# One product for the last FFN chunk's 64 gate rows and 64 up rows, with ScalarE moving the up rows to the gate rows' partitions

## The reference, cut to what matters

```python
g = jnp.einsum('td,edf->tef', x, wg)          # 32 experts, 96 hidden each
u = jnp.einsum('td,edf->tef', x, wu)
act = jax.nn.silu(g) * u
routed = jnp.einsum('tef,efd,te->td', act, wd, combine)
shared = jax.nn.silu(hidden_states @ sg) * (hidden_states @ su) @ sd   # 192 hidden
return routed + shared
```

## Time and the profile before

| | |
|---|---|
| median of 3 runs | 1710.79 us (1708.7 to 1717.45) |
| the profiled execution | 1712.23 us, of which its span is 1710.4 us |
| mean granted TensorE clock in it | 0.955 |
| PE busy | 1536.3 us |
| DVE busy | 1258.4 us |
| POOL busy | 982.6 us |
| ACT busy | 844.5 us |

### The profile page before, as it was taken

One profiled execution on the slowest core, in us unless ns is written; L12 is line 12 of the kernel. 1 busy time (PEld: TensorE's weight loads), 2 busy tenths in 40 slices (PEclk: granted clock), 3 DMA queues, 4 the chain that ended last, 5 costly groups with the idle time before them and its releaser, 6 DMA issues. The chain is left out here.

```text
span 1710.4 us, 22495 instructions
## 1 busy us (share of the span) xinstructions
PE 1536.3 (90%) x7088; PEld 1165.2 (68%) x7088; DVE 1258.4 (74%) x2067; ACT 844.5 (49%) x1692; POOL 982.6 (57%) x1048
## 2 busy tenths in 40 slices
PE   5998798888899989897999898989996999799979
PEld 4665555556666667776777777767775777577868
DVE  4553688877878688888988888888877887777321
ACT  3443565543565346545663465446534564444233
POOL 0653365654766457655765575557644776478335
PEclk7999998999999999999999999989997999899989
DMA  5565321223423324333324333324332433243334
GB/s 168 203 234 174 107 86 62 70 79 107 139 93 105 101 94 135 114 118 117 111 96 138 102 131 113 111 99 132 124 101 68 137 113 122 75 139 132 125 113 142
DMA packets 73430, 202.35 MB, mean 118 GB/s; under 512 B 10049, under 2 KB 22561, under 8 KB 72929
## 3 DMA queue, kind: packets, MB, share of 16 engines
q1 hardware_dynamic: 65120, 175.75, 30.9%
q0 software_dynamic: 8192, 25.17, 4.9%
HBM read 175.46 MB, written 25.43 MB: 117 GB/s over the span
## 5 line engine op out<-in xcount | busy, mean ns | idle before, releaser
L842 PE MATMUL gub<-x_hi,wr 128*128 128x384 f32 (+2 forms) x1040 | 424.8, 408 | 36.5 <-DVE hid L1209 29.1
L1512 POOL TENSOR_TENSOR ring<-ring 128x512 f32<-128x512 f32 x192 | 254.6, 1326 | 313.1 <-DVE ring L1392 312.9
L923 PE MATMUL acc<-hid,w_down 128*128 128x384 f32 (+2 forms) x1040 | 401.4, 511 | 1.0 <-POOL hid L1491 0.8
L1491 POOL TENSOR_TENSOR hid<-hid,u_sb 128x384 f32<-128x384 f32 (+2 forms) x260 | 286.0, 1100 | 196.2 <-ACT u_sb L1075 180.7
L843 PE MATMUL gub<-x_lo,wr 128*128 128x384 f32 (+2 forms) x1040 | 370.8, 357 | 0.0
L844 PE MATMUL gub<-x_hi,wr 128*128 128x384 f32 (+2 forms) x1040 | 370.8, 357 | 0.0
L1386 DVE TENSOR_TENSOR_SCAN ring<-decays,side 128x512 f32<-128x512 f32 x256 | 310.5, 1213 | 19.2 <-ACT decays L1173 16.0
L1085 ACT ACTIVATE hid<-gub 128x384 f32<-128x384 f32 (+2 forms) x324 | 156.9, 484 | 308.7 <-PE gub L844 154.4
L1075 ACT ACTIVATE u_sb<-gub 128x384 f32<-128x384 f32 (+2 forms) x260 | 132.4, 509 | 325.6 <-PE gub L844 325.2
L1499 POOL TENSOR_TENSOR hid<-hid,weight 128x384 f32<-128x384 f32 (+2 forms) x240 | 269.2, 1122 | 26.3 <-ACT weight L1065 10.7
L923 PEld LDWEIGHTS acc<-hid,w_down 128*128 128x128 f32 x1040 | 187.0, 191 | 95.5 <-issue 41.6
(11 more groups left out here) (116 smaller groups left out, 1785.7 us busy)
## 6 DMA issues: line engine op xcount, KB each, us to landing
wr<-w_halves SPq DMA_DIRECT2D x234, 512.0 KB, 3.3
wm_gu<-in_w_mlp POOLq DMA_DIRECT2D x64, 256.0 KB, 3.1
w_halves<-wr SPq DMA_DIRECT2D x26, 512.0 KB, 4.1
wm_down<-in_w_mlp POOLq DMA_DIRECT2D x64, 128.0 KB, 2.7
w_raw<-in_w_gu SPq DMA_DIRECT2D x26, 256.0 KB, 4.0
rows<-parts SPq DMA_DIRECT2D x16, 384.0 KB, 2.3
cst<-rows SPq DMA_DIRECT2D x48, 128.0 KB, 2.6
xin<-in_x SPq DMA_DIRECT2D x8, 256.0 KB, 2.9
```

The costliest lines, as they stand in the source:

```text
L842: mm(out, w[:, 0, half, k, :], x_hi[:, k, a:b], start=(k == 0), stop=False)
L923: last = mm(acc[k][:, a:b], w, h[:, a:b], start=(c == 0), stop=(c == (MLP_CHUNKS if mlp else FFN_CHUNKS) - 1))
L1491: nc.gpsimd.tensor_tensor(h, h, u_sb[c % USLOTS][:, a:b], ALU.mult).then_inc(sem["hidden"], 1)
L1512: add(ysum, ysum, ring[:, ring_at(it)], ALU.add).then_inc(sem["y_sum"], 1)
```

## The change

The 64 gate rows and the 64 up rows of chunk 25 now lie in one weight tile of 128 columns. On the host the up columns of the shared expert's last 64 rows take the place of the padding in the gate tile, and the up tile of this chunk is zero. TensorE makes one product for chunk 25: its PSUM bank then has the gate on partitions 0 to 63 and the up rows on partitions 64 to 127. ScalarE takes the tanh of partitions 0 to 63 as before and, in the place in its list where the up copy was, copies partitions 64 to 127 to partitions 0 to 63 of `u_sb`. The bank may not be refilled before both have read it, and it is VectorE's gate product whose end frees it; so VectorE now waits for the copy as well (`u_copied`) before it runs `by_g` of chunk 25. The element-wise work of this chunk and its down product use 64 partitions; their free sizes are as before. The weight load by DMA still moves the whole tile, zeros too.

```diff
+REST = FSH % P
...
+    "u_last": {"u_copied": 1},
...
+    if item[0] == "u" and item[2] == FFN_CHUNKS - 1:
+        return "u_last"
...
-                    sp.wait_ge(sem["u_filled"], s.count("u_filled", ("u", "ff", before), 1))
+                    if before == FFN_CHUNKS - 1:
+                        sp.wait_ge(sem["g_filled"], s.count("g_filled", ("g", "ff", before), 1))
+                    else:
+                        sp.wait_ge(sem["u_filled"], s.count("u_filled", ("u", "ff", before), 1))
...
-                elif kind == "u":
+                elif kind == "u" and it[2] < FFN_CHUNKS - 1:
                     for over, least in s.last_use("gub", it):
                         pe.wait_ge(sem[over], least)
                     glu_half(s, it, 1).then_inc(sem["u_filled"], 1)
...
+                    r = REST if not mlp and c == FFN_CHUNKS - 1 else P
                     for k in range(KC):
-                        w = wm_down[c % MSLOTS][:, k, :] if mlp else w_down[:, c, k * P:(k + 1) * P]
-                        last = mm(acc[k][:, a:b], w, h[:, a:b], start=(c == 0),
+                        w = wm_down[c % MSLOTS][:, k, :] if mlp else w_down[0:r, c, k * P:(k + 1) * P]
+                        last = mm(acc[k][:, a:b], w, h[0:r, a:b], start=(c == 0),
...
+                    if c == FFN_CHUNKS - 1:
+                        A(u_sb[c % USLOTS][0:REST, a:b], s.gub_of(("g", "ff", c))[P - REST:P, a:b],
+                          ACT.Copy).then_inc(sem["u_copied"], 1)
+                    else:
+                        A(u_sb[c % USLOTS][:, a:b], s.gub_of(it)[:, a:b], ACT.Copy).then_inc(sem["u_copied"], 1)
...
                     dve.wait_ge(sem["tanh_done"], s.count("tanh_done", of, 1))
-                    v.scalar_tensor_tensor(h, h, 1.0, s.gub_of(of)[:, a:b], ALU.add,
+                    if c == FFN_CHUNKS - 1:
+
+                        dve.wait_ge(sem["u_copied"], s.count("u_copied", ("u", "ff", c), 1))
+                    v.scalar_tensor_tensor(h, h, 1.0, s.gub_of(of)[0:r, a:b], ALU.add,
                                            ALU.mult).then_inc(sem["gated"], 1)
...
+    w_gu[-1, :, 0, :, REST:], w_gu[-1, :, 1] = w_gu[-1, :, 1, :, 0:REST], 0.0
```

More of the change, by code:

```diff
@@ L1069, in do @@
                     a, b = spans[s.n]
-                    act.wait_ge(sem["u_filled"], s.count("u_filled", it, 1))
+                    if c == FFN_CHUNKS - 1:
+                        act.wait_ge(sem["g_filled"], s.count("g_filled", ("g", "ff", c), 1))
+                    else:
+                        act.wait_ge(sem["u_filled"], s.count("u_filled", it, 1))
                     if c >= USLOTS:
@@ L1074, in do @@
                         act.wait_ge(sem["hidden"], least)
-                    A(u_sb[c % USLOTS][:, a:b], s.gub_of(it)[:, a:b], ACT.Copy).then_inc(sem["u_copied"], 1)
+                    if c == FFN_CHUNKS - 1:
+                        A(u_sb[c % USLOTS][0:REST, a:b], s.gub_of(("g", "ff", c))[P - REST:P, a:b],
+                          ACT.Copy).then_inc(sem["u_copied"], 1)
+                    else:
+                        A(u_sb[c % USLOTS][:, a:b], s.gub_of(it)[:, a:b], ACT.Copy).then_inc(sem["u_copied"], 1)
                 elif kind in ("g", "gum"):
@@ L1084, in do @@
                         act.wait_ge(sem["down_done"], least)
-                    A(hid[c % HSLOTS][:, a:b], s.gub_of(it)[:, a:b], ACT.Tanh,
+                    r = REST if kind == "g" and c == FFN_CHUNKS - 1 else P
+                    A(hid[c % HSLOTS][0:r, a:b], s.gub_of(it)[0:r, a:b], ACT.Tanh,
                       scale=0.5).then_inc(sem["tanh_done"], 1)
@@ L1205, in do @@
                     a, b = spans[s.n]
-                    h = hid[c % HSLOTS][:, a:b]
+                    r = REST if c == FFN_CHUNKS - 1 else P
+                    h = hid[c % HSLOTS][0:r, a:b]
                     of = ("g", "ff", c)
                     dve.wait_ge(sem["tanh_done"], s.count("tanh_done", of, 1))
-                    v.scalar_tensor_tensor(h, h, 1.0, s.gub_of(of)[:, a:b], ALU.add,
+                    if c == FFN_CHUNKS - 1:
+                        dve.wait_ge(sem["u_copied"], s.count("u_copied", ("u", "ff", c), 1))
+                    v.scalar_tensor_tensor(h, h, 1.0, s.gub_of(of)[0:r, a:b], ALU.add,
                                            ALU.mult).then_inc(sem["gated"], 1)
@@ L1487, in do @@
                     a, b = spans[s.n]
-                    h = hid[c % HSLOTS][:, a:b]
+                    r = REST if c == FFN_CHUNKS - 1 else P
+                    h = hid[c % HSLOTS][0:r, a:b]
                     pool.wait_ge(sem["u_copied"], s.count("u_copied", ("u", "ff", c), 1))
                     pool.wait_ge(sem["gated"], s.count("gated", ("by_g", "ff", c), 1))
-                    nc.gpsimd.tensor_tensor(h, h, u_sb[c % USLOTS][:, a:b], ALU.mult).then_inc(sem["hidden"], 1)
+                    nc.gpsimd.tensor_tensor(h, h, u_sb[c % USLOTS][0:r, a:b], ALU.mult).then_inc(sem["hidden"], 1)
                 if it[0] == "by_comb":
```

## The result

The changed kernel takes 1717.4 us (median of 19 runs, 1710.32 to 1729.76). The kernel before took 1708.7 us in 19 runs beside it (1702.11 to 1717.45). The ratio is 1.0057, 95% interval [1.0043, 1.0072]: some 10 us slower, at the edge of the 0.5% that I called no change, with the interval on both sides of it. Three executions of 3.1 to 8.6 ms among those of the experiments are left out of the ratios. The profiled execution took 1717.08 us, its span 1715.3 us, at a mean granted clock of 0.957.

The account below looks back on a forecast made before the run. At most step ends TensorE and VectorE were taken to run as one chain. Step terms summed to +3.8 us, with +1.5 for the clock +5.3: 1717.5 against the profiled 1712.2; from the 1710.8 median, forecast 1716 us, range 1705 to 1722.

Parts of the forecast that it names:

- The price of a matmul and the ceiling: Six matmuls fewer per step: 1.4, 1.1 or 0.8 us for 512, 384 or 256 columns; at most 11.6 us gained.
- Steps 0 and 9: Ends of steps 0 and 9: the removed matmuls' saving counts in full, -1.4 and -0.8 us.
- Step 1: End of step 1: by_g waits for the late copy, delaying scan and B product, +3.3 us.
- the term of the clock: Behind step 1's new 4.6 us TensorE gap: another stretch at reduced clock, +1.5 us.
- my example: Windows 394 to 398 before the change, after one without matmuls: clock 0.50 and 0.78, losing 1.4 us.
- Step 4: End of step 4: by_g after the copy delays the xn_mlp multiplies, scan and C product, +1.2 us.
- slower by half clock after each gap: Rival: each idle TensorE stretch at step ends brings half clock, 1.5 us each; 1720.6 us with four; chance 0.13.
- Steps 2 and 6: Ends of steps 2 and 6: by_g, then GpSimd's product and the last down product come later, +0.8 and +1.2 us.
- Steps 3, 5 and 7: Ends of steps 3, 5, 7: scans hold TensorE in 3 and 5, GpSimd waits for by_g in 7; 0 each.
- Step 8: End of step 8: GpSimd's product ends at 1604.8, leaving about 0.5 of 1.1 us saved, -0.5 us.
- full gain: Rival: the copy wait is covered everywhere and TensorE's saving counts in each step; 1699 us, chance 0.07.
- No net effect: Rival: slack in the following step absorbs VectorE's delays; 1708 to 1710 us, chance 0.2.

Follow-up runs that it names:

- the product kept: Changed kernel without VectorE's wait, TensorE making six unread matmuls where the up product was: 1.0019 against the kernel before; with 128 down-product rows 1.0000.
- The first seven experiments: Wait alone, early copy, no wait, early copy without wait, product kept, merging in three steps, wait in step 1 alone: ratios 1.0008 to 1.0091.
- the last five: Down product over 128 rows without wait, with product kept, in three steps, in the changed kernel; over 64 in the kernel before: 0.9974 to 1.0049.
- the early copy: Changed kernel with chunk 25's copy directly behind its tanh, VectorE's wait kept: 1.0042 against the kernel before.
- both: Changed kernel with chunk 25's copy directly behind its tanh and without VectorE's wait for it: 1.0030 against the kernel before.
- the best version: Changed kernel without VectorE's wait, last chunk's down product over all 128 rows: 0.9974 against the kernel before, median 1703.31 us.

## Why the prediction was right, and where not

**The price of a matmul and the ceiling** stand: the page's count fell by 60, and where a product's time counts in full and nothing else changes, as in steps 0 and 9 with the down product over 128 rows, the ends moved by -1.4 and -0.7 against my 1.4 and 0.8. That the busy time fell by 11.7 us, beside my 11.6, is no confirmation: it changes with the clock of the execution. The kernel before had 1536.3 us, and the one with the product kept and 128 rows, with as many matmuls, 1527.2.

**Steps 0 and 9** (forecast -1.4 and -0.8, measured -1.2 and -0.5). The savings counted in full, as claimed, but I had written that the down product costs nothing new. There are 0.33 us of idle time ahead of its last four weight loads, those over 64 rows, and the end is 0.2 us later for it. With 128 rows the ends are -1.4 and -0.7. The product alone over 64 rows gives the same +0.2.

**Step 1** (forecast +3.3 and +1.5 for the clock, measured +6.3). The mechanism was that of the forecast link by link: `by_g` behind the copy, the scan behind `by_g`, the B product behind the scan. From the tanh to the B product it was 378.97 - 374.52 = 4.45 us before and 381.87 - 373.86 = 8.01 us after, +3.6 against my +3.3. The rest, 2.7 us, is the term of the clock, which I had sized at 1.5 by an example with two slow windows. Here the three windows from 382 to 388 lose 2 x (0.50 + 0.50 + 0.25) = 2.5 us by the same reckoning. TensorE is busy without a gap there, so the longer multiplies on VectorE have no part in it. The stretch of my example is gone in this trace: from 394 to 400 the clock is 1.00. I had taken the length of the slow stretch from one place and had no reason for it to be the same elsewhere. The wait alone in step 1 confirms both parts together (+5.1; there the up product still fills some of the gap).

**Step 4** (forecast +1.2, measured +4.0). This is the term of the sum that failed. The changed kernel's rows, against the earlier trace rows:

```profile
931.46 0.49 ACT L1088 ACTIVATE u_sb<-gub 64x384 f32<-64x384 f32 x1
...
932.04 0.55 DVE L1230 SCALAR_TENSOR_TENSOR hid<-hid,gub 64x384 f32<-64x384 f32 x1 [2.11 <-ACT u_sb L1088]
932.51 1.60 DVE L1302 SCALAR_TENSOR_TENSOR xn_mlp<-hn,lnw,rstd 128x256 f32<-128x256 f32 x2
...
932.73 1.10 POOL L1513 TENSOR_TENSOR hid<-hid,u_sb 64x384 f32<-64x384 f32 x1 [2.54 <-DVE hid L1230]
...
935.30 0.39 PE L1029 MATMUL side<-cst,sel_c 96*128 96x256 bf16 x2 [3.08 <-DVE ring L1407]
```

Two things were missed. First, before, GpSimd's product had to wait for the late copy, which ended after the two multiplies into `xn_mlp`. Now copy, `by_g` and multiplies follow each other closely, so that GpSimd's product, which waited for `by_g`, runs at the same time as the multiplies, and they take 1.60 us and not 0.88. Second, TensorE's gap had grown to 3.08 us, where I had reckoned with 2.3, and it too was followed by half clock:

```profile
934.00:936.00 2.00, 0.70 (x4) 0.56 (x5) 1.90 (x4) 0.00 (x0) 0.00 (x0) 1.00 0.00 0
936.00:938.00 2.00, 2.00 (x5) 0.74 (x4) 1.86 (x3) 0.00 (x0) 1.26 (x1) 0.64 0.00 0
938.00:940.00 2.00, 2.00 (x4) 0.67 (x2) 0.69 (x1) 0.00 (x0) 1.18 (x1) 0.50 0.00 0
```

Those windows lose (0.36 + 0.50) x 2 = 1.7 us. Not every such gap has it: in the trace of the changed kernel with 128 rows in the down product, the gap of step 4 is as long, the multiplies take 1.60 us too, and the clock stays at full:

```profile
926.27 0.39 PE L1029 MATMUL side<-cst,sel_c 96*128 96x256 bf16 x2 [3.09 <-DVE ring L1407]
```

```profile
926.00:928.00 2.00, 1.73 (x7) 1.17 (x8) 1.81 (x4) 0.00 (x0) 0.92 (x1) 1.00 0.00 0
928.00:930.00 2.00, 1.43 (x6) 0.59 (x5) 1.90 (x4) 0.00 (x0) 0.56 (x2) 1.00 0.00 0
```

The end of step 4 is +2.5 there and not +4.0. So of the 2.8 us over my +1.2, about 1.3 belong to the longer multiplies (0.7) and small shifts around them, and the other 1.5 (with 0.2 for the 64 rows) to a stretch of half clock that only one of these two executions shows. The rival "slower by half clock after each gap" had named steps 1 and 4 at 1.5 us each; it was right on these two places in the changed kernel's trace. Of the other ends only step 6's showed a little of it (a granted clock of 0.72 from 1277 to 1279, where the step's last addition starts at 1278.36). That rival and the forecast were thus mixed in the outcome.

**Steps 2 and 6** (+0.8 and +1.2, measured +1.3 and +1.5): the mechanism was right, and the size to 0.5 and 0.3 us. **Steps 3, 5 and 7** (0): right; the kernel with the product kept and the one without differ there by nothing, so six matmuls are worth nothing at these ends.

**Step 8** (-0.5, measured 0): mis-sized. In the changed kernel GpSimd's product started 5.66 us behind the tanh where my hand-overs gave 5.4, took 1.10 us, and the last down product waited for it. By the kernel without the wait step 8 gives -0.6.

The other rivals: full gain fell by the wait alone and by the kernel without the wait, which keeps 2.7 of 11.6 us. No net effect fell with the time and with the wait in step 1 alone, whose whole +7 us is no less than its end. But what this rival said of slack behind a step is true of one place. Behind step 1 TensorE waits for the MLP's weights. In the kernel before and in the changed one:

```profile
392.56 2.91 PE L884 MATMUL gub<-xn_mlp,wm_gu 128*128 128x256 f32 x8 [2.68 <-DMA wm_gu<-in_w_mlp]
...
428.83 0.74 DVE L1239 SCALAR_TENSOR_TENSOR x<-acc,res 128x256 f32<-128x256 f32 x2
```

```profile
395.92 1.99 PE L892 MATMUL gub<-xn_mlp,wm_gu 128*128 128x256 f32 x8 [1.28 <-DMA wm_gu<-in_w_mlp]
...
431.05 0.74 DVE L1260 SCALAR_TENSOR_TENSOR x<-acc,res 128x256 f32<-128x256 f32 x2
```

The last rows are the addition at the end of step 2's MLP. From the tanh of chunk 25 in step 1 it is 54.31 us before and 57.19 us after: of the 6.3 us that step 1's end lost, 2.9 are left there, and 3.0 in the changed kernel with 128 rows. The trace of the wait in step 1 alone does not show this: +5.1 at the end is +6.5 at the same addition.

I had named step 1, the copy and VectorE's order, and these carried the result. The median lies 1.4 us from my number. That it lies so near is partly luck. The ends' sum is 6.0 us above my +5.3 (step 4 has 2.8 of it, step 1 with the clock 1.5, steps 2 and 8 0.5 each). But the kernel before took 1708.7 us over 19 runs where I had started from 1710.8, and the medians moved by 2.6 us less than the ends (8.7 against 11.3): 1716.1 + 6.0 - 2.1 - 2.6 = 1717.4.

**What stays open.** The first seven experiments lay 2 to 7 us above what their ends say (for instance 1.4 over before with ends of -2.7), the last five within 1.2 us of them. The seven were compared on two chips, the five on two others. The kernel without the wait had a mean granted clock of 0.957 (12 runs) with 64 rows in the down product and of 0.962 (12 runs) with 128. I suspected the 64 rows. Against them speak three things: alone in the kernel before they cost 1.0 us, if with a wide interval; taken out of the changed kernel they won back nothing certain; and the two kernels with a wait added to the kernel before, which have 128 rows, lay 4.1 and 1.9 us above their ends as well. Whether the excess belongs to the chips, or to something in these kernels that only some executions show, was not settled, since none but the kernel before was timed on both pairs. Some of it may lie where the ends don't look. In the traces of the three kernels of the first pair that lack the product and don't lose 6 us at step 1 (the early copy, no wait, both), TensorE's wait for the MLP's weights behind step 1 is 3.95 to 4.19 us long and not 2.68, and the addition at the end of that MLP comes 2.1 to 2.4 us later than their ends say; all three also have half clock around the end of step 2, where the kernel before has none. But the best version has the longer wait too (3.53 us, 1.3 us later) without an excess. Why the weights come later was not looked into. The excess bears on the size of the gain of the best version too: its interval reaches from 0.9 to 7.9 us, and its twin with 64 rows showed none.

## What to carry to other kernels

Before merging two producers into one buffer, look at who frees the buffer: a wait on the release, put on the engine whose next instruction is a scan in a long chain, cost 15 us by itself, while the buffer was already protected by a later wait on TensorE that everybody had to pass. Price a removed product at the places where TensorE ends last; here that was four of ten step ends, 3.3 us of 11.6. Where an edit opens a gap on TensorE, reckon with half clock behind it as one case of two: it stood behind gaps of 2.68, 3.08, 3.27 and 4.79 us here, and in step 6 behind two of 1.66 and 1.39, but not behind one of 3.09. Then ask which instructions of VectorE and GpSimd now fall together, and whether what follows the late place waits for something else anyway.

## What was not expected of the hardware

The first weight load with 64 rows behind loads with 128 starts later than another load would: in step 9 its row shows 0.33 us idle ahead of it, and the step's end is 0.2 us later, in the product-kept kernel and in the kernel before with 64 rows alone. With 128 rows of which 64 are zeros it goes away, so the zeros were the cheaper choice.

VectorE's two multiplies into `xn_mlp` take 0.88 us alone and 2.51 us in step 1 of the changed kernel, where GpSimd had already begun. GpSimd's rows there:

```profile
382.69 1.26 POOL L1534 TENSOR_TENSOR ring<-ring 128x512 f32<-128x512 f32 x1 [5.33 <-DVE ring L1413]
383.91 1.44 POOL L1513 TENSOR_TENSOR hid<-hid,u_sb 64x512 f32<-64x512 f32 x1
```

The multiplies run from 383.12 to 385.63, and GpSimd's two from 382.69 to 385.35: each of the two multiplies (1.11 and 1.48 us long by the trace) ends some 0.3 us after one of GpSimd's. The Trainium skill (SBUF — State Buffer, SBUF: two separate sides) states that a VectorE instruction with two SBUF inputs and a GpSimd one that reads SBUF contend for a shared pair of ports, and that the one which starts first has it for the whole instruction while the other waits. The rows fit it: GpSimd's had started first both times, and neither multiply ended before GpSimd's instruction had. No experiment moved GpSimd's work alone, so the cause is argued and not shown.

ScalarE read partitions 64 to 127 of a PSUM bank and wrote 0 to 63 of SBUF in 0.59 us, as long as the copy in place (0.58).
